# Values as the stationary operand, turned back bank by bank, in an attention and expert block on one core

## What is computed

```python
q = split_heads(hidden_states @ Wq, q_len)
k = split_heads(hidden_states @ Wk, q_len)
v = split_heads(hidden_states @ Wv, q_len)
q = q * cos + _rotate_half(q) * sin
k = k * cos + _rotate_half(k) * sin
scores = jnp.einsum('bhqd,bhkd->bhqk', q, k) * inv_sqrt_d + attention_mask
w = jax.nn.softmax(scores, axis=-1)
attn_output = jnp.einsum('bhqk,bhkd->bhqd', w, v)
a_scores = jnp.einsum('bhqd,bhkd->bhqk', q, a_k) * inv_sqrt_d
a_scores = jnp.tanh(gate) * jax.nn.softmax(a_scores, axis=-1)
attn_output = attn_output + jnp.einsum('bhqk,bhkd->bhqd', a_scores, a_v)
x = x + attn_output @ Wo
x = x + moe(_layernorm(x))     # router: top 2 of 8, then w1, silu * up, w2
```

## Time and profile before

| | |
|---|---|
| median of 3 runs | 2759.8 us |
| lowest and highest | 2749.01, 2766.76 us |
| profiled execution | 2745.8 us |
| its span | 2744.1 us |
| mean granted clock of TensorE | 0.848 of full |

### The profile page before, as it was taken

One profiled execution on the slowest core, in us unless ns is written; L12 is line 12 of the kernel. 1 busy time (PEld: TensorE's weight loads), 2 busy tenths in 40 slices (PEclk: granted clock), 3 DMA queues, 4 the chain that ended last, 5 costly groups with the idle time before them and its releaser, 6 DMA issues. The chain is left out here.

```text
span 2744.1 us, 55286 instructions
## 1 busy us (share of the span) xinstructions
PE 2365.1 (86%) x18441; PEld 1716.4 (63%) x18442; DVE 1376.3 (50%) x4993; ACT 1199.3 (44%) x2132; POOL 854.6 (31%) x883
## 2 busy tenths in 40 slices
PE   4999998888788987888788888988888918999997
PEld 2776666666566765666566666766666715666664
DVE  4465555555455544555556565655565333333332
ACT  3555444444344443454345454544444214444433
POOL 2213322223222222222222222222233133444443
PEclk7998878788788888898889898888898658999999
DMA  2010000000000000010001010000001204444444
GB/s 93 23 48 27 27 27 27 26 27 27 27 27 27 27 27 7 25 43 28 10 27 36 26 41 27 27 27 27 27 23 18 40 26 97 85 84 83 82 82 67
DMA packets 69872, 106.45 MB, mean 39 GB/s; under 512 B 25024, under 2 KB 29120, under 8 KB 69120
## 3 DMA queue, kind: packets, MB, share of 16 engines
q0 software_dynamic: 24096, 37.51, 7.9%
q1 hardware_dynamic: 45536, 65.69, 7.8%
HBM read 67.51 MB, written 35.65 MB: 38 GB/s over the span
## 5 line engine op out<-in xcount | busy, mean ns | idle before, releaser
L1089 PE MATMUL av<-vv,pr 128*128 128x17 f32 x4096 | 617.8, 287 | 6.0 <-issue 5.7
L1089 PEld LDWEIGHTS av<-vv,pr 128*128 128x128 f32 x4096 | 609.6, 227 | 19.9 <-issue 5.9
L519 ACT ACTIVATE pr<-st 128x512 f32<-128x512 f32 x512 | 305.0, 596 | 588.9 <-PE st L1075 444.7
L699 DVE TENSOR_REDUCE mx<-md 128x4 f32<-128x512 f32 x256 | 176.7, 690 | 343.8 <-remote 223.8
L1043 PE MATMUL md<-kk,qz 128*128 128x128 f16 x2048 | 212.4, 252 | 149.3 <-DVE mx L699 92.6
L1407 PE MATMUL y<-w1s,hgT 128*128 x1704 | 280.3, 315 | 4.7 <-ACT hgT L1321 4.7
L417 POOL DMA_INDIRECT lists<-row,posi x256 | 249.0, 973 | 86.2 <-issue 86.2
L1043 PEld LDWEIGHTS md<-kk,qz 128*128 128x128 f16 x2048 | 154.6, 114 | 182.0 <-issue 129.3
L702 DVE CUSTOM_DVE_ANT_0 md<-md,msk 128x128 f32<-128x128 f32 x1024 | 264.9, 321 | 0.0
L403 POOL TENSOR_TENSOR avs<-avs,rc 128x512 f32<-128x512 f32 x32 | 34.6, 1083 | 658.3 <-DVE rc L734 658.3
L1066 PE MATMUL st<-qz,kk 128*128 128x256 f16 x1024 | 211.9, 291 | 30.0 <-issue 22.4
(11 more groups left out here) (198 smaller groups left out, 3850.8 us busy)
## 6 DMA issues: line engine op xcount, KB each, us to landing
wst<-in_w SPq DMA_DIRECT2D x32, 352.0 KB, 3.6
cin<-in_ctx SPq DMA_DIRECT2D x32, 256.0 KB, 4.0
xin<-in_x SPq DMA_DIRECT2D x32, 256.0 KB, 3.8
xres<-in_x SPq DMA_DIRECT2D x32, 256.0 KB, 3.4
out<-x SPq DMA_DIRECT2D x32, 256.0 KB, 2.1
h_pairs<-ohs SPq DMA_DIRECT2D x32, 256.0 KB
lists<-row,posi POOLq DMA_INDIRECT x256
msk<-in_mask SPq DMA_DIRECT2D x32, 64.0 KB, 3.2
```

What stands on the lines that cost most here:

```text
L519: act.activation(pr[:, path, :, :], st[path][:, :, :], ACT.Exp).then_inc(p_ex.sem, 1)
L699: dve.tensor_reduce(mx[:, 1, 4 * g:4 * g + 4], sm[1][:, :, :], AX.X, ALU.max).then_inc(s_ad.sem, 1)
L1089: i = pe.matmul(av[g // 2 % 2][:, h % 8, path, :], pr[:, path, j, :], vv[:, n.par, path, h, :], start=True, stop=True)
```

## The change

The value matmuls trade operands: a head's values with the ones (128x17) become stationary and its exponentials (128x128) move. The result stands transposed, 17 partitions by 128 queries, and the four heads of a set go to partitions 0, 32, 64 and 96 of one bank. After four sets ACT copies the bank to `avT` (`values_T`), PE turns its four parts back into the same bank by fp32 transposes (`values_back`), and DVE normalizes it from PSUM (`normal`): reciprocal, gate, one product of both paths, one sum into `on`. `values_out`, `norm_out`, `own_out` and `sum_out` go.

In `maxima` the four fused operations become one add of the mask over four heads and one reduce. The orders are new on every engine: `places` in unit 5 and bank `ma[0]`, the turns of o and the context after the values of unit 3, `values` ahead of the scores' pieces, `values_back` in units 6, 10, 14 and after `avp`, `router_rows` split off `router_weights`, POOL's `w_slice` behind `norm_h`. The diff, cut to its core:

```diff
@@ -168,7 +171,7 @@
 
 
     st = [ps(f"st{k}", [P, 4, P], F32) for k in range(2)]
-    av = [ps(f"av{k}", [P, 8, 2, VW], F32) for k in range(2)]
+    av = [ps(f"av{k}", [P, 4, P], F32) for k in range(2)]
     ma = [ps(f"ma{k}", [P, 512], F32) for k in range(2)]
     md = [ps(f"md{k}", [P, 512], F32) for k in range(2)]
     sm = [bank[:, :].rearrange("p (a n) -> p a n", a=4) for bank in md]
...
@@ -518,6 +514,12 @@
             act.wait_ge(av_pe.sem, av_pe.at(n, u - 1))
             act.activation(pr[:, path, :, :], st[path][:, :, :], ACT.Exp).then_inc(p_ex.sem, 1)
 
+        def values_T(n, o):
+
+            act.wait_ge(av_pe.sem, av_pe.at(n, 4 * o + 4))
+            act.wait_ge(v_back.sem, v_back.at(n, o))
+            act.activation(avT[:, :, :], av[o % 2][:, :, :], ACT.Copy).then_inc(v_T.sem, 1)
+
         def w_slice(n):
             act.wait_ge(w_in.sem(n), w_in.at(n))
             act.activation(slice_of(n, 0), wst[:, :], ACT.Copy, scale=WS)
...
@@ -644,6 +653,8 @@
 
         pool_c_all = 19
         dve.wait_ge(pool_c.sem, pool_c_all)
+        for bank in av:
+            dve.memset(bank[:, :, :], 0.0)
         dve.tensor_copy(ident16[:, :], identf[:, :]).then_inc(dve_c.sem, 1)
         dve.tensor_copy(identr[:, :], identf[:, :]).then_inc(dve_c.sem, 1)
         dve.tensor_copy(ident_bf[:, :], identf[:, :]).then_inc(dve_c.sem, 1)
@@ -697,13 +708,12 @@
             dve.wait_ge(s_pe.sem, s_pe.at(n, g + 1))
             dve.wait_ge(s_own.sem, s_own.at(n, g))
             dve.tensor_reduce(mx[:, 1, 4 * g:4 * g + 4], sm[1][:, :, :], AX.X, ALU.max).then_inc(s_ad.sem, 1)
-            for j in range(4):
-                h = 4 * g + j
-                i = dve.tensor_tensor_reduce(sm[0][:, j, :], sm[0][:, j, :], msk[:, n.par, :], 1.0, -3.4028235e38,
-                                             ALU.add, ALU.max, mx[:, 0, h:h + 1])
-            i.then_inc(s_own.sem, 1)
-
-        def neg_max(n):
+            dve.tensor_tensor(sm[0][:, :, :], sm[0][:, :, :], msk[:, n.par, :].unsqueeze(1).to_broadcast([P, 4, P]),
+                              ALU.add).then_inc(s_mask.sem, 1)
+            dve.wait_ge(s_mask.sem, s_mask.at(n, g + 1))
+            dve.tensor_reduce(mx[:, 0, 4 * g:4 * g + 4], sm[0][:, :, :], AX.X, ALU.max).then_inc(s_own.sem, 1)
+
+        def neg_max(n, b=None):
 
             dve.wait_ge(s_own.sem, s_own.at(n))
             dve.wait_ge(s_ad.sem, s_ad.at(n))
@@ -719,38 +729,31 @@
             dve.tensor_tensor(mr[:, :, :], mr[:, :, :], p3[1], ALU.subtract).then_inc(m_part.sem, 1)
             dve.wait_ge(m_part.sem, m_part.at(n, 4))
             dve.tensor_copy(p3[2], mr[:, :, :]).then_inc(mp3.sem, 1)
+            if b:
+                normal(b, 3)
             dve.wait_ge(mp_t.sem, mp_t.at(n))
             dve.tensor_copy(mT[:, :, :], m_bank()[0:3 * NH]).then_inc(m_T.sem, 1)
 
-        def values_out(n, o):
-            dve.wait_ge(av_pe.sem, av_pe.at(n, 4 * o + 4))
+        def normal(n, o):
+
+            bank = av[o % 2][:, :, :].rearrange("p (a g) (j c) -> p a (g j) c", a=2, c=VC)
+            dve.wait_ge(v_back.sem, v_back.at(n, o + 1))
+            dve.reciprocal(rc[:, :, :], bank[:, :, :, HD]).then_inc(n_rc.sem, 1)
+            dve.wait_ge(n_rc.sem, n_rc.at(n, o + 1))
+            dve.tensor_tensor(rc[:, 1, :], rc[:, 1, :], tg[:, 8 * o:8 * o + 8], ALU.mult).then_inc(n_rg.sem, 1)
+            dve.wait_ge(n_rg.sem, n_rg.at(n, o + 1))
+            dve.tensor_tensor(part2[:, :, :, :], bank[:, :, :, 0:HD],
+                              rc[:, :, :].unsqueeze(3).to_broadcast([P, 2, 8, HD]), ALU.mult).then_inc(n_o2.sem, 1)
+            dve.wait_ge(n_o2.sem, n_o2.at(n, o + 1))
             if o == 0:
-                dve.wait_ge(n_o.sem, n_o.at(n.shift(-1)))
-            dve.tensor_copy(avs[:, 8 * o:8 * o + 8, :, :], av[o % 2][:, :, :, :]).then_inc(av_s.sem, 1)
-
-        def norm_out(n):
-
-            dve.wait_ge(av_s.sem, av_s.at(n))
-            dve.reciprocal(rc[:, :, :], avs[:, :, :, HD]).then_inc(n_rc.sem, 1)
-            dve.wait_ge(n_rc.sem, n_rc.at(n))
-            dve.tensor_tensor(rc[:, :, 1], rc[:, :, 1], tg[:, :], ALU.mult).then_inc(n_rg.sem, 1)
-            dve.wait_ge(n_rg.sem, n_rg.at(n))
-            dve.tensor_tensor(avs[:, :, 1, 0:HD], avs[:, :, 1, 0:HD],
-                              rc[:, :, 1:2].to_broadcast([P, NH, HD]), ALU.mult).then_inc(n_o2.sem, 1)
-
-        def sum_out(n, x_batch):
-            if x_batch:
-                dve.wait_ge(x_hi.sem, x_hi.at(x_batch))
-                dve.wait_ge(x_lo.sem, x_lo.at(x_batch))
-            dve.wait_ge(n_o1.sem, n_o1.at(n))
-            dve.wait_ge(n_o2.sem, n_o2.at(n))
-            dve.wait_ge(h_hi.sem, h_hi.at(n.shift(-1)))
-            dve.wait_ge(h_lo.sem, h_lo.at(n.shift(-1)))
-            dve.tensor_tensor(heads(nat), avs[:, :, 0, 0:HD], avs[:, :, 1, 0:HD], ALU.add).then_inc(n_o.sem, 1)
+                dve.wait_ge(o_hi.sem, o_hi.at(n.shift(-1)))
+                dve.wait_ge(o_lo.sem, o_lo.at(n.shift(-1)))
+            dve.tensor_tensor(heads(on)[:, 8 * o:8 * o + 8, :], part2[:, 0, :, :], part2[:, 1, :, :],
+                              ALU.add).then_inc(n_o.sem, 1)
 
         def out_low(n):
             dve.wait_ge(o_hi.sem, o_hi.at(n))
-            dve.tensor_tensor(ohs[:, 1, :], nat[:, :], ohs[:, 0, :], ALU.subtract).then_inc(o_lo.sem, 1)
+            dve.tensor_tensor(ohs[:, 1, :], on[:, :], ohs[:, 0, :], ALU.subtract).then_inc(o_lo.sem, 1)
 
         def residual(n):
             dve.wait_ge(o_p.sem, o_p.at(n))
@@ -812,9 +816,9 @@
         def router_counts(n):
 
             dve.wait_ge(f_p.sem, f_p.at(n))
-            dve.tensor_tensor(pos[:, :], md[1][:, 0:NE], count[:, :], ALU.add).then_inc(f_c.sem, 1)
+            dve.tensor_tensor(pos[:, :], ma[0][:, 0:NE], count[:, :], ALU.add).then_inc(f_c.sem, 1)
             dve.wait_ge(f_c.sem, f_c.at(n))
-            dve.tensor_tensor(count[:, :], md[1][:, NE:2 * NE], count[:, :], ALU.add).then_inc(f_cnt.sem, 1)
+            dve.tensor_tensor(count[:, :], ma[0][:, NE:2 * NE], count[:, :], ALU.add).then_inc(f_cnt.sem, 1)
 
         def router_weights(n):
 
@@ -846,30 +853,28 @@
 
         def step(b, c, d, n, m):
             if d:
-                norm_out(d)
-                sum_out(d, n)
+                out_low(d)
             if n:
                 ctx_lo(n)
                 mask_lo(n)
-            if d:
-                out_low(d)
-            if n:
                 rotate_q(n)
             if c:
                 router_top(c)
-                router_counts(c)
             if n:
                 rotate_k(n)
             if c:
                 router_weights(c)
-            values_out(b, 0)
             if d:
                 residual(d)
-                norm_h(d)
+                norm_h(d, n)
+            if c:
+                router_counts(c)
+                router_rows(c)
+            if d:
                 h_low(d)
             if n:
                 ak_low(n)
-            values_out(b, 1)
+            normal(b, 0)
             if d:
                 router_logits(d)
             if m:
@@ -880,15 +885,17 @@
                 norm_x(m)
             if n:
                 maxima(n, 1)
-                maxima(n, 2)
-            values_out(b, 2)
+            normal(b, 1)
             if n:
-                for g in range(3, 7):
+                for g in range(2, 5):
                     maxima(n, g)
-            values_out(b, 3)
+            normal(b, 2)
             if n:
-                maxima(n, 7)
-                neg_max(n)
+                for g in range(5, 8):
+                    maxima(n, g)
+                neg_max(n, b)
+            else:
+                normal(b, 3)
 
         def first(n):
             rotate_q(n)
...
@@ -1083,12 +1091,19 @@
                 pe.wait_ge(av_v.sem, av_v.at(n))
                 pe.wait_ge(v_v.sem, v_v.at(n))
             if u % 4 == 0:
-                pe.wait_ge(av_s.sem, av_s.at(n, u // 4 - 1))
+                pe.wait_ge(n_o.sem, n_o.at(n, u // 4 - 1))
             for j in range(4):
                 h = 4 * g + j
-                i = pe.matmul(av[g // 2 % 2][:, h % 8, path, :], pr[:, path, j, :], vv[:, n.par, path, h, :],
-                              start=True, stop=True)
+                i = pe.matmul(av[u // 4 % 2][VC * j:VC * j + VW, 2 * path + g % 2, :], vv[:, n.par, path, h, :],
+                              pr[:, path, j, :], start=True, stop=True)
             i.then_inc(av_pe.sem, 1)
+
+        def values_back(n, o):
+
+            pe.wait_ge(v_T.sem, v_T.at(n, o + 1))
+            for k in range(4):
+                i = pe.transpose(av[o % 2][:, k, :], avT[:, k, :], identf[:, :])
+            i.then_inc(v_back.sem, 1)
 
         def out_turn(n):
             pe.wait_ge(o_hi.sem, o_hi.at(n))
@@ -1110,43 +1123,54 @@
             pe.wait_ge(h_T.sem, h_T.at(n))
             project(md[1], hT, rw, NE).then_inc(r_p.sem, 1)
 
-        def places(n):
+        def places(n, ctx_batch=None):
 
```

(65 more changed lines are left out.)

62 lines of the change are left out of this document (26 added, 36 removed).

## The result

The changed kernel takes 2528.0 us, median of 4 runs (2524.06 to 2539.28), the kernel before 2760.1 beside it (2749.01 to 2766.76): a ratio of 0.917 (95%: 0.913 to 0.921), 232 us. The forecast was 2640 with a range of 2500 to 2780. The side and the range hold, the range because it reaches over rival A; the forecast's own range (2570 to 2710) misses. It saw half of the gain, and the time is nearly that of rival A (2520).

What follows compares the result with a forecast made beforehand. PE busy 86% of the span; within a step PE bound part 1, PE and DVE paced part 2. Terms -5.4, +0.6, +1.3 made -3.5 us per step, 116 in all: 2640 us, own range 2570 to 2710, wider 2500 to 2780.

Steps and rivals of the forecast that it cites:

- rival A: Heads side by side and the clock holds: a set at 0.25 us, -7.5 us per step, 2520 us; chance 17%.
- Part 1: Step from the mT copy to the next batch's first scores, 30.9 us before: 25.5 after, DVE-bound, -5.4.
- the turn: PE's four fp32 transposes of 128x128, four times a step: 0.5 us each time, 2 us of PE per step.
- the normalization: DVE's new reciprocal, product, PSUM product, add and four waits, four times a step: 1.25 us each.
- the set: Value matmuls of four heads on PE: 0.45 us instead of 0.87, 0.9 at half clock; 6.7 us per step less.
- The drain at a change of tiling mode: TensorE draining when tiling mode changes: forecast would lose 2.4 us in Part 1, up to that in Part 2.
- B: A set of values costs what it did: -0.6 us per step, 2735 us (2700 to 2785); chance 22%.
- Part 2: Step from first to eighth scores, 26.6 us before: 25.2 plus 2 for half clock, 27.2, so +0.6.
- the unnamed wait: DVE's wait in Part 2 for something the trace can't name, 5.84 us in the step: as long as before.
- Part 3: v, avp, turns and next mT copy, 9.2 us before: fourth turn back 0.5, last normalization 0.8, +1.3.
- The last step and what follows: Last step, which has no next batch: -7 us; the expert phase left alone by the change.
- The maxima: DVE's add and reduces replacing four fused operations: 2.07 us against 1.70, +0.37 per group; 2.56 against 2.19 with waiting.

Runs made afterwards that it cites:

- e2: The kernel before with only places moved to unit 5 and the router's counts and rows put behind norm_h: 2404.6 us, ratio 0.956 to before.
- e6: The change with the four heads of a set in one column group instead of four, normalization product in two instructions: 2717.0 us, ratio 0.986 to before.
- e8: The kernel before, unchanged, traced on a chip of the first kind (before takes some 2756 us): 2743.7 us, clock 0.848.
- e1: The kernel before with only the values: stationary values, ACT's copy and the turn back: 2339.1 us, ratio 0.928 to before.
- e10: The change with the four fused maxima of before put back, beside e9 on one chip: 2307.3 us, ratio 0.918 to before.
- e9: The change as it is, on a chip of the second kind (before takes some 2517 us): 2349.6 us, ratio 0.934 to before.
- e3: The kernel before with only the two-instruction maxima (one mask add, one reduce) in place of four fused operations: 2550.6 us, ratio 1.013 to before.
- e7: The change with POOL entering the lists (eight scatters) ahead of the lower part of x: 2580.3 us, ratio 0.936 to before.
- e11: The change with POOL's list scatters moved to the start of the next step: 2521.5 us, ratio 1.002 to before, 7.3% above e9.
- e12: The change with both the fused maxima and the scatters at the start of the next step: 2441.2 us, ratio 0.971 to before.

## Why the forecast was right, and where it was too cautious

**Part 1: right.** It is where most of the gain lies: 5.4 of the 8.1 us in this step. Forecast 25.5 us, bound by DVE; it took 25.5 (1470.82 to 1496.27), places without a wait. Four of the terms can be read off: the set 0.35 where I took 0.45, the turn 0.44 for 0.5, the normalization 1.23 (1493.60 to 1494.83) for 1.25, w_o 2.76. The sum ended on DVE, so the error in the set cost nothing here.

**The set: mis-sized, between forecast and A.** e6 shows that the low price comes from heads side by side. The Trainium skill's 2.38x for three column tiles (TensorE: Matmul & The Clock Gate, Part 3) gave an estimate of 0.37; with four, e6 and the change give 0.98/0.35, 2.8. That 0.37 came so near is in part luck: it divided the 0.87 of the old sets, which load 128 columns, and not the 0.98 of the new ones standing one behind another, which is what the factor compares. The drain at a change of tiling mode (the Trainium skill, TensorEngine Tiling, Key Properties) is not seen apart in any run; whatever there is of it lies inside the 0.35, so B is out.

**Part 2: the step that failed.** I wrote that PE would work about 2.0 us of every 2.8 and that "this is the share at which its clock fell before", and added 2 us for half clock: 27.2. It took 24.7 (1496.27 to 1521.00). PE worked even less than that, 1.75 of 3 us, and the clock stood at 1.00; before, 2.15 of 3 was followed by 0.67. Without the +2 the sum was 25.2. PE's busy share in such a window does not tell whether the clock falls: e2 kept 1.00 behind 2.03 of 3 us. Nor do the runs show that it is the columns moved, 17 or 128. e6 (128 columns, 0.938) against e8 (17 columns, 0.848) would speak for it, but e2, with 17 columns, has 0.922 to 0.943 in its runs where before has 0.889 to 0.906 on that chip, and e1, with 128, has no more than 0.940. In the steps shown of both kernels part 2's fall came inside the unnamed wait, while PE had little to do; over all steps 13 of 29 falls of part 2 lie in such a wait before, 25 of 36 in the change. What decides the others stays open. Where the clock did fall, a unit at half clock cost little, since the set was 0.56 then and not the 0.9 that I took from doubling.

**Part 3: the same step again.** Forecast 10.5, it took 8.45 (1521.00 to 1529.45): I left v at half clock, A did not (-2.4). The turn was 0.44 for 0.5, the last normalization 1.16 up to the copy for 0.8. Together the step is 58.6 where the forecast's terms give 63.2.

**From one step to the sum.** That step fell by 8.1 us, the mean only by 6.65: the step shown is one of the short ones, and some have a second unnamed wait. 31 times 6.65 are 206. The last step and what follows is 19.0 shorter, against 7. That comes with the values: behind the last copy e1 takes 571.7 us, e2 590.7 on the same chip. That 2528 came out so near to A's 2520 is in part luck: A's own terms (-5.4, -1.4 and -1.1) make -7.9 a step and 2508, not the -7.5 that I wrote, its set was 0.25, and it had the 7 for the end.

**The maxima.** +0.37 per group on DVE was nearly right (2.51 against 2.19 in e10, 0.32) and showed as time lost; I had it under a total that fell for other reasons. Over 31 steps of eight groups it would be 79 us; e9 less e10 is 42, e3 less before 32. Where the rest is taken up was not tried.

**The parts don't add.** On the chips without the wait, values alone bring 7.2%, places alone 4.4%, both in the new order with the fused maxima 8.2% (e10), and the change as it is 6.6% (e9), no more than the values alone. The means of the 31 steps, cut at the mT copy and at the first and eighth maximum, show where the rest stays: e1 takes 31.8, 16.5 and 6.4 us, e10 27.5, 18.6 and 7.2. The new order of e10, with places and the normalization gone from the head of the step, is 4.2 shorter in part 1; parts 2 and 3 are 2.9 longer. Three of the four normalizations now stand in them, 1.15 us each (the row from 1516.29), where e1 has a copy.

**The unnamed wait.** I forecast it "as long as before", and it is (218.9). But it is worth more to before: 239 us (2755.6 less 2516.5) against 176 (2526.0 less 2349.6). So of the 230 us between the two on the first kind of chip, 63 come from meeting that pause better, and where it is absent the change is worth 167 (ratio 0.934). The traces show where: in the median of the 31 steps the two last groups behind the wait are 4.0 and 4.2 us apart in e8, with sets at half clock, and 2.7 and 2.7 in the change. These 2.8 us a step, some 85 in all, are enough for it. That they are the 63 is argued: before has no trace on a chip without the wait.

**What stays open.** Why DVE gets on late while POOL issues scatters, and why on some chips only. That the place of the wait follows the scatters is shown by e7; that a better place would win its 176 us was not shown, e11 having met two waits of its own. There is a second kind of unnamed wait: nine steps of the change have one of 2.5 to 7.4 us (40 in all) that ends 9 to 14 us behind the last scatter. The 26.7 us of e9 are nearly all of this kind, so both kinds of chip have it, and in e11 and e12, whose scatters stand elsewhere, DVE has no such wait at all. What it belongs to was not tried. The fastest kernel here is the change with the fused maxima (2307.3, ratio 0.918 on its chip, where the change is at 0.934); on a chip with the wait it wasn't run.

## What to carry to other kernels

When a matmul's result is narrow, make the narrow operand stationary and give neighbours different groups of 32 columns, if the partitions are free for it: the groups were worth 191 us here, and without them the whole bundle kept 1.4% of its 8.3%. Undo each part of a bundle by itself: this one carried a loss of 1.8% under a gain of 8%. Before moving a queue's long stretch of DMA issues, list what stands behind it on that queue and who rewrites its source: in e11 each was a wait of 7 us in a step. And don't forecast the clock from one pair of neighbouring windows: the run that would have spoken against it here was the smallest edit, e2.
